# A mixture-of-experts layer on one core: the second product set between the halves of the next expert's first product, and requests held until scatters are issued

## The chip, the cores and the metric

The kernel runs on one core of a Trainium2 chip. The metric is device time in microseconds (us). Times of the kernel before are given as the median of three runs and as one profiled execution.

## The reference

A gated cross-attention block is followed by a gated mixture of experts over 2048 tokens of 256 elements. The change touches the second part alone:

```
logits = xf @ gate_w.T;  probs = sigmoid(logits)
top_vals, sel = top_k(probs, 2)                      # 2 of 16 experts a token
weights = top_vals / (top_vals.sum(-1) + 1e-6)
slot = expert * capacity + rank                      # capacity 320 rows an expert
padded[slot] = x_rep                                 # rows of each expert
h = gelu(einsum('ecd,edf->ecf', padded, w1))         # first product: 256 -> 512
out_padded = einsum('ecf,efd->ecd', h, w2)           # second product: 512 -> 256
out = (out_padded[slot] * weights).sum over the 2 choices
x = x + tanh(g_ffn) * out
```

## The kernel before, in words

Every engine has a program of its own, written out by hand, and semaphores alone tie them together. The first part (attention, router) writes each token's normalised row to the DRAM tensor `padded`, at the place of its expert and rank, with indirect DMAs issued by GpSimd (`dispatch`, L456 to L461). The expert part then loops over e = -4 to 15 on each engine (`expert_steps`, L319), where a step works on several experts at once.

All products take float32 operands in two parts, a high one (rounded to float32r) and a low one (the rest), and sum three of the four partial products (`PARTS`, L1201). So a 128 x 128 block of weights costs three matmuls.

**SyncE** (L371 to L399) asks for the data. `fetch(e)` issues three DMAs for the 320 rows of an expert (into `xg`, which stands in the tile `diag`, 5 buffers). In step e it asks for w2 of expert e + 3 (once the buffer `raw2` is free: w2_low), then w1 of e + 4 (w1_low), then fetches the rows of e + 3. Each waits in order on the one queue. A weight request is 512 KB.

**TensorE** (L1345 to L1419). `first_product` of step e belongs to expert e + 1: four blocks f of the 512 hidden elements, each with 2 x 3 matmuls into its own PSUM bank of `ps_scores`, 24 weight loads (L1370) in all. Ahead of f = 0 and of f = 2 it waits until the results of the expert before have left the first or second two banks (h_low; per expert it counts 2, one a half). `turn` (L1354) transposes the rows of e + 2 in six steps. `second_product` of expert e goes over the rows in three tiles: k = 0 and k = 1 of 128 rows, 12 matmuls each (L1388), and the third of 64 rows (L1398, L1399). It waits for w2_low, for both halves of h (h_low at 2e + 2), and for its output banks (y_last, y_ready). For expert 15 the output goes to banks of `ps_scores` instead.

**ScalarE** (L703 to L750) in step e: gelu of the two halves of e + 1 in place (L713), high part of the rows of e + 2 (L701), high part of w1 of e + 3 (L723), result k = 0 of e scaled by its weight into `y` (the tile `wqT`, L729), high part of w2 of e + 2 (L741), result k = 1 (L729), half of the third (L747). `rows_high`, `result` and `rows_low` are its and VectorE's helpers.

**VectorE** (L1081 to L1121) in step e: for each half of h of e + 1 a high part (L1093) and two low parts (L1095, L1096; the last raises h_low), low part of the rows (L1079), of w1 of e + 3 (L1106; raises w1_low), of w2 of e + 2 (L1110; raises w2_low), and the third result (L1118; raises y_last).

**GpSimd** (L545 to L555) adds the results into the output with indirect DMAs that accumulate, one for each k. Before an expert's first it waits until all three of the expert before have landed (`added`), since two experts may hold the same token; then each waits for its result (y_ready, y_ready, y_last). A memset of one column, `sent`, marks the end of the dispatches (L540).

Of the kernel before, what the change touches and what calls it, by code (L numbers as in the profile page):

```python
# [5 lines left out]
F32 = mybir.dt.float32  # L6
# [58 lines left out]
def exists(t, n=TILES):  # L65

    return 0 <= t < n
# [8 lines left out]
def build(nc, x, ctx_in, mask, g_xattn, g_ffn, ln_gamma, ln_beta, wq, wkv, wo, bo, gate_w, w1, w2, out):  # L76
# [8 lines left out]
    with ExitStack() as held:  # L85
# [36 lines left out]
        sent = sb("sent", [P, 1])  # L122
# [131 lines left out]
        gate_centred, rows_sent = sem("gate_centred"), sem("rows_sent")  # L254
# [61 lines left out]
        def dispatch_done(engine, r):  # L316
            engine.wait_ge(dispatched[r % 2], 64 * (r // 2 + 1))

# [5 lines left out]
        def _(sp):  # L324
# [61 lines left out]
            def expert(e, j, i):  # L386

                n = e + 3
# [3 lines left out]
                n = e + 4  # L392
                if 2 <= n < EXPERTS:
                    sp.wait_ge(w1_low, n - 1)
                    sp.dma_start(raw1[:, n % 2], w1_load[n]).then_inc(w1_loaded[n % 2], 16)
                if e >= -1:
                    fetch(e + 3)
# [4 lines left out]
        def _(pool):  # L402
# [137 lines left out]
            pool.memset(sent[:, :], 0.0).then_inc(rows_sent, 1)  # L540
# [4 lines left out]
            for e in range(EXPERTS):  # L545
# [15 lines left out]
        def _(act):  # L561
# [141 lines left out]
            def expert(e, j, i):  # L703
# [5 lines left out]
                t = e + 1  # L709
                if exists(t, EXPERTS):  # L710
                    for h in range(2):
                        act.wait_ge(h_made, 2 * t + h + 1)
                        act.activation(h_at(t, h), ps_scores[:, 2 * h:2 * h + 2, 0:CAPACITY], ACT.Gelu).then_inc(h_act, 1)  # L713
                if e >= 0:
                    rows_high(e + 2, j)

                t, p = e + 3, (j + 1) % 2
                if exists(t, EXPERTS):
                    act.wait_ge(w1_loaded[p], 16 * (t // 2 + 1))
                    wait(act, h_made, 2 * (t - 1))  # L720
                    if t < 2:
                        act.wait_ge(scored, 2 * TILES)
                    act.activation(w1_hl(p, 0), raw1[:, p], ACT.Copy).then_inc(w1_high, 1)  # L723
# [29 lines left out]
        def _(dve):  # L753
# [327 lines left out]
            def expert(e, j, i):  # L1081
# [5 lines left out]
                t, p = e + 1, (j + 1) % 2  # L1087
                if exists(t, EXPERTS):
                    for h in range(2):
                        fs, n = slice(2 * h, 2 * h + 2), 2 * P  # L1090
                        dve.wait_ge(h_act, 2 * t + h + 1)
                        wait(dve, y_made, SLOT_TILES * (t - 1))
# [9 lines left out]
                if exists(t, EXPERTS):  # L1102
                    if t == 0:
                        dve.wait_ge(rows_sent, 1)
# [338 lines left out]
```

## Time and profile before

| What | us |
| --- | --- |
| Median of 3 runs | 340.29 |
| Range of the runs | 338.02 to 340.69 |
| Profiled execution, device time | 339.9 |
| Its span | 338.2 |
| TensorE busy (matmul) | 308.3 |
| TensorE weight loads busy | 267.3 |
| VectorE busy | 251.2 |
| ScalarE busy | 207.9 |
| GpSimd busy | 191.4 |

The span runs from the first to the last recorded instruction; the device time has 1.7 us more around it. Matmuls (PE) are pipelined and recorded with modelled ends, so the weight loads (PEld), which follow one another, show TensorE's pace better. SPq and POOLq are DMA issues. A timeline row merges like instructions that follow each other (x24). `wqT` is the tile of the results `y`, `diag` that of the gathered rows, `score_t` and `w_third` hold the split weights, `value_t` the split rows and h.

### The profile page before, as it was taken

What the parts mean: (1) busy time and instruction counts of PE and PEld (TensorE: products, weight loads), DVE (VectorE), ACT (ScalarE), POOL (GpSimd) and SP (SyncE); (2) the same over time, 40 slices, a digit from 0 to 9 for tenths busy, and PEclk for the clock granted to TensorE, in tenths of its full rate; (3) what the DMA queues carried; (4) which work ended last, traced back from release to release, by engine and by line L of the source; (5) the groups of instructions that cost most, each with busy time, mean ns of one, the idle gap of its engine ahead of it and who ended that gap; (6) DMA issues with size and microseconds to landing.
All of it is one profiled execution on the core that took longest, in us unless ns stands there. A gap on an engine that the chain in (4) does not pass through costs nothing. (4 is left out here: it accounts for less than half of the span.)

```text
span 338.2 us, 6265 instructions
## 1 busy us (share of the span) xinstructions
PE 308.3 (91%) x2077; PEld 267.3 (79%) x2080; DVE 251.2 (74%) x585; ACT 207.9 (61%) x570; POOL 191.4 (57%) x242
## 2 busy tenths in 40 slices
PE   8989999999999999998849999999999999999800
PEld 3646779988888888887724899999999999999700
DVE  2679887698989898989755398888888888887200
ACT  2646877887888888866461376666666666665300
POOL 8034566585777777788771023555555555566650
PEclk9999999999999999999978999999999999999965
DMA  6989999700111111111224737878787878853440
GB/s 159 274 241 292 182 167 152 195 19 16 49 49 55 57 57 64 56 51 62 78 95 149 249 104 201 204 205 208 204 216 211 224 202 220 211 82 43 48 46 8
DMA packets 40906, 45.68 MB, mean 135 GB/s; under 512 B 5461, under 2 KB 34666, under 8 KB 40874
## 3 DMA queue, kind: packets, MB, share of 16 engines
q1 hardware_dynamic: 33410, 35.78, 39.3%
q0 software_dynamic: 7424, 9.48, 15.6%
q8 instruction: 17, 0.28, 0.4%
q14 instruction: 15, 0.12, 0.2%
q10 hardware_dynamic: 40, 0.02, 0.0%
HBM read 28.02 MB, written 17.24 MB: 134 GB/s over the span
## 5 line engine op out<-in xcount | busy, mean ns | idle before, releaser
L554 POOL DMA_INDIRECT out_dram<-wqT,diag x48 | 73.3, 1528 | 77.4 <-DMA out_dram<-wqT,diag 43.4
L1370 PE MATMUL ps_scores<-value_t,score_t 128*128 128x320 f32 x384 | 59.1, 310 | 0.0
L1370 PEld LDWEIGHTS ps_scores<-value_t,score_t 128*128 128x128 f32 x384 | 56.5, 188 | 0.4 <-DVE value_t L1079 0.3
L1269 PE MATMUL ps_out<-value_t,pT 128*128 128x256 f32 x384 | 53.3, 289 | 0.9 <-DVE pT L968 0.9
L1240 PE MATMUL ps_scores<-score_t,xn 128*128 128x512 f32 x192 | 53.9, 426 | 0.0
L1269 PEld LDWEIGHTS ps_out<-value_t,pT 128*128 128x128 f32 x384 | 47.7, 189 | 1.7 <-issue 1.6
L1240 PEld LDWEIGHTS ps_scores<-score_t,xn 128*128 128x128 f32 x192 | 36.4, 190 | 6.8
L713 ACT ACTIVATE ps_scores<-ps_scores 128x640 f32<-128x640 f32 x30 | 20.6, 688 | 34.2 <-PE ps_scores L1370 34.1
L460 POOL DMA_INDIRECT padded<-z,slot_row x32 | 33.4, 1043 | 10.0 <-issue 7.1
L640 ACT ACTIVATE probs<-ps_scores,row_low 128x64 f32<-128x64 f32 x128 | 38.0, 327 | 0.5 <-DVE row_low L941 0.5
L1093 DVE CAST value_t<-ps_scores 128x640 fp32r<-128x640 f32 x30 | 24.7, 824 | 18.0 <-ACT ps_scores L713 17.8
L492 POOL TENSOR_TENSOR probs<-probs,norm 128x1024 f32<-128x1024 f32 x15 | 28.6, 1906 | 5.5 <-DVE norm L909 5.5
L640 ACT ACTIVATION_READ_ACCUMULATOR probs<-ps_scores,row_low 128x1 f32 x128 | 28.4, 222 | 0.0
L848 DVE TENSOR_TENSOR pT<-ps_pT,pT 128x512 fp32r<-128x512 f32 x28 | 18.5, 660 | 5.2 <-ACT pT L606 4.9
L1095 DVE TENSOR_TENSOR value_t<-ps_scores,value_t 128x512 fp32r<-128x512 f32 x30 | 20.8, 692 | 1.0
L1106 DVE TENSOR_TENSOR score_t<-raw,score_t 128x1024 fp32r<-128x1024 f32 x16 | 19.4, 1216 | 2.6 <-POOL sent L540 2.6
L1193 PE MATMUL ps_misc<-zeros 128*128 128x512 bf16 x62 | 18.8, 461 | 1.5 <-DVE zeros L805 1.2
L1079 DVE TENSOR_TENSOR value_t<-ps_pT,value_t 128x640 fp32r<-128x640 f32 x16 | 13.1, 816 | 8.2 <-ACT value_t L701 8.2
L606 ACT ACTIVATE pT<-ps_pT 128x512 fp32r<-128x512 f32 x32 | 18.0, 644 | 0.9 <-PE ps_pT L1217 0.9
L701 ACT ACTIVATE value_t<-ps_pT 128x640 fp32r<-128x640 f32 x16 | 11.3, 706 | 11.9 <-PE ps_pT L1354 11.7
L630 ACT ACTIVATE gexp<-ps_scores,l 128x16 f32<-128x16 f32 x16 | 4.4, 276 | 22.3 <-PE ps_scores L1256 16.7
L483 POOL CAST xn<-xn_full 128x256 fp32r<-128x256 f32 x16 | 6.4, 399 | 20.6 <-ACT xn_full L654 20.5
(210 smaller groups left out, 690.0 us busy)
## 6 DMA issues: line engine op xcount, KB each, us to landing
raw<-in_L_ffn_w_dram SPq DMA_DIRECT2D x16, 512.0 KB, 4.8
wo_sb<-in_L_ffn_w_dram SPq DMA_DIRECT2D x16, 512.0 KB, 3.5
padded<-empty SPq DMA_DIRECT2D x2, 2064.0 KB, 31.0
diag<-padded SPq DMA_DIRECT2D x16, 258.0 KB, 4.9
out_dram<-x SPq DMA_DIRECT2D x16, 128.0 KB, 1.7
padded<-empty SPq DMA_DIRECT2D x1, 1032.0 KB, 34.1
diag<-padded SPq DMA_DIRECT2D x16, 64.5 KB, 4.7
wq_sb<-in_L_xattn_Wq_dram SPq DMA_DIRECT2D x2, 512.0 KB, 8.0
```

What stands on the lines that cost most here:

```text
L460: pool.indirect_dma_start(padded, bass.IndirectOffsetOnAxis(ap=slot_row[:, r % 2, k, q:q + 1], axis=0), z2[:, (2 * r + k) % RING, q], None ...
L492: pool.tensor_tensor(probs[:, p], probs[:, p], norm[:, p, :, None].to_broadcast([P, HEADS, KEYS]), ALU.mult).then_inc(normed, 1)
L554: pool.indirect_dma_start(out, bass.IndirectOffsetOnAxis(ap=xg[0:SLOTS[k], r, k, TOKEN:TOKEN + 1].bitcast(U32), axis=0), y[0:SLOTS[k], j, ...
L640: op = act.activation(probs[:, j, n], ps_scores[:, 1, at:at + KEYS], ACT.Exp, scale=-1.0, bias=row_low[:, n:n + 1], accum_out=row_sum[:, j ...
L713: act.activation(h_at(t, h), ps_scores[:, 2 * h:2 * h + 2, 0:CAPACITY], ACT.Gelu).then_inc(h_act, 1)
L1093: dve.tensor_copy(h_high_of(p)[:, fs], h_at(t, h)).then_inc(h_high, 1)
L1095: dve.tensor_tensor(h_low_of(p)[:, fs], h_at(t, h)[:, :, 0:n], h_high_of(p)[:, fs, 0:n].bitcast(F32), ALU.subtract)
L1106: dve.tensor_tensor(w1_hl(p, 1), raw1[:, p], w1_hl(p, 0).bitcast(F32), ALU.subtract).then_inc(w1_low, 1)
L1193: pe.matmul(ps_misc[:, :], idle_rows[:, 0:P], idle_rows, start=True, stop=True)
L1240: op = pe.matmul(dst, xn[:, t % 2, a, c], mv, start=False, stop=last)
L1269: op = pe.matmul(ps_attn, pT[:, a, c], mv, start=c == 0 and (a, b) == PARTS[0], stop=c == HC - 1 and (a, b) == PARTS[-1])
L1370: op = pe.matmul(ps_scores[:, f, 0:CAPACITY], w1_hl(p, a)[:, c, f * P:(f + 1) * P], x_hl(p, b)[:, c], start=c == 0 and (a, b) == PARTS[0], ...
```

## The change

- TensorE: for e = 0 to 13 the step is now blocks f = 0, 1 of the first product of e + 1, the turn of e + 2, the second product of e, blocks f = 2, 3 of e + 1. Step 14 does the whole first product of 15 and then the second product of 14; step 15 the second product of 15. The second product starts once the first half of h is split, and asks for the second half ahead of k = 0, f = 2. For expert 15 the waits on y_last and y_ready are gone.
- ScalarE and VectorE: the order of the halves follows (`halves`): half 1 of e, then w1 of e + 2, then half 0 of e + 1, the rows, and so on.
- GpSimd: after an expert's three scatters it writes one column of `sent` and raises a new semaphore, `issued` (experts 0 to 14).
- SyncE: from step 1 on, the rows of e + 3 are fetched first, and only once expert e - 1's scatters are issued; then w1 of e + 4, then w2 of e + 3. In steps before that w1 stands ahead of w2, and the rows last.

```diff
-        sent = sb("sent", [P, 1])
+        sent = sb("sent", [P, EXPERTS])
...
+        def halves(e):
+
+            if e == -1:
+                return ((0, 0), (0, 1))
+            mine = ((e, 1),) if 0 < e < EXPERTS - 1 else ()
+            later = ((e + 1, 0),) if 0 <= e < EXPERTS - 1 else ()
+            return mine + later + (((e + 1, 1),) if e == EXPERTS - 2 else ())
...
             def expert(e, j, i):      # SyncE
 
+                if e >= 1:
+                    sp.wait_ge(issued, e)
+                    fetch(e + 3)
+                n = e + 4
+                if 2 <= n < EXPERTS:
+                    sp.wait_ge(w1_low, n - 1)
+                    sp.dma_start(raw1[:, n % 2], w1_load[n]).then_inc(w1_loaded[n % 2], 16)
                 n = e + 3
                 if 2 <= n < EXPERTS:
                     sp.wait_ge(w2_low, n - 1)
                     sp.dma_start(raw2[:, n % 2], w2_load[n]).then_inc(w2_loaded[n % 2], 16)
-                n = e + 4
-                if 2 <= n < EXPERTS:
-                    sp.wait_ge(w1_low, n - 1)
-                    sp.dma_start(raw1[:, n % 2], w1_load[n]).then_inc(w1_loaded[n % 2], 16)
-                if e >= -1:
+                if -1 <= e < 1:
                     fetch(e + 3)
...
-            pool.memset(sent[:, :], 0.0).then_inc(rows_sent, 1)
+            pool.memset(sent[:, EXPERTS - 1:], 0.0).then_inc(rows_sent, 1)
...
+                if e < EXPERTS - 1:   # GpSimd, behind an expert's three scatters
+                    pool.memset(sent[:, e:e + 1], 0.0).then_inc(issued, 1)
...
+                def first_high(t, p):      # ScalarE
+
+                    if exists(t, EXPERTS):
+                        act.wait_ge(w1_loaded[p], 16 * (t // 2 + 1))
+                        wait(act, h_made, 2 * (t - 1))
+                        if t < 2:
+                            act.wait_ge(scored, 2 * TILES)
+                        act.activation(w1_hl(p, 0), raw1[:, p], ACT.Copy).then_inc(w1_high, 1)
+
+                for t, h in halves(e):
+                    act.wait_ge(h_made, 2 * t + h + 1)
+                    act.activation(h_at(t, h), ps_scores[:, 2 * h:2 * h + 2, 0:CAPACITY], ACT.Gelu).then_inc(h_act, 1)
+                    if e > 0 and t == e:
+                        first_high(e + 2, j)
                 if e >= 0:
                     rows_high(e + 2, j)
+                else:
+                    first_high(e + 3, (j + 1) % 2)
...
-                    pe.wait_ge(h_low, 2 * e + 2)
+                    pe.wait_ge(h_low, 2 * e + 1)
                     for k in range(SLOT_TILES - 1):
-                        if k == 0:
-                            wait(pe, y_last, e)
-                        else:
-                            wait(pe, y_ready, 2 * e)
+                        if e < EXPERTS - 1:
+                            if k == 0:
+                                wait(pe, y_last, e)
+                            else:
+                                wait(pe, y_ready, 2 * e)
                         for f in range(FC):
+                            if k == 0 and f == FC // 2:
+                                pe.wait_ge(h_low, 2 * e + 2)
...
+                elif e < EXPERTS - 2:
+                    first_product(e, j, i, range(FC // 2))
+                    turn(e, j, i)
+                    second_product(e, j, i)
+                    first_product(e, j, i, range(FC // 2, FC))
                 else:
                     first_product(e, j, i)
-                    turn(e, j, i)
                     second_product(e, j, i)
```

VectorE's part changes as ScalarE's does: `first_low` (L1106's split, with the same waits) stands behind half 1 of e, and in steps before 0 at the end of the halves.

## Rows read from the trace of the kernel before

**Rows 1.** The page's slices: busy tenths of TensorE in 40 equal slices.

```profile
PE   8989999999999999998849999999999999999800
```

**Rows 2.** Busy time by stretch: us, each engine (count), PEclk, DMA share, GB/s.

```profile
250.00:260.00 10.00, 10.00 (x78) 9.76 (x77) 8.59 (x13) 6.26 (x11) 4.55 (x3) 1.00 0.75 184
...
330.00:338.00 8.00, 0.00 (x0) 0.00 (x0) 0.00 (x0) 0.00 (x0) 0.00 (x0) 0.50 0.05 6
```

**Rows 3.** Who waited for whom, 195 to 325 us: total us, times, longest.

```profile
POOL out_dram L554 <- DMA out_dram<-wqT,diag: 43.4, 15, 5.5
...
PE ps_scores L1388 <- DVE wqT L1118: 1.3, 1, 1.3
```

**Rows 4.** Timeline, one period of the weight loads: start us, us, engine, line, operation.

```profile
250.56 3.53 PEld L1370 LDWEIGHTS ps_scores<-value_t,score_t 128*128 128x128 f32 x24
...
254.99 1.49 PEld L1388 LDWEIGHTS ps_out<-score_t,value_t 128*128 128x128 f32 x12
...
258.79 3.53 PEld L1370 LDWEIGHTS ps_scores<-value_t,score_t 128*128 128x128 f32 x24
```

**Rows 5.** Timeline: the last split of the results of that first product.

```profile
256.59 0.28 DVE L1096 TENSOR_TENSOR value_t<-ps_scores,value_t 128x128 fp32r<-128x128 f32 x1
```

**Rows 6.** Timeline of GpSimd, first to last scatter: [idle before, releaser].

```profile
178.37 0.12 POOL L540 MEMSET sent<- 128x1 f32 x1
...
200.63 1.62 POOL L554 DMA_INDIRECT out_dram<-wqT,diag  x1 [22.14 <-ACT wqT L729]
...
202.55 2.03 POOL L554 DMA_INDIRECT out_dram<-wqT,diag  x1 [0.31 <-issue]
...
260.78 1.56 POOL L554 DMA_INDIRECT out_dram<-wqT,diag  x1 [3.18 <-DMA out_dram<-wqT,diag]
...
286.00 1.56 POOL L554 DMA_INDIRECT out_dram<-wqT,diag  x1 [3.92 <-DMA out_dram<-wqT,diag]
...
304.97 1.42 POOL L554 DMA_INDIRECT out_dram<-wqT,diag  x1 [0.31 <-issue]
...
308.79 1.56 POOL L554 DMA_INDIRECT out_dram<-wqT,diag  x1 [2.40 <-DMA out_dram<-wqT,diag]
...
316.51 1.56 POOL L554 DMA_INDIRECT out_dram<-wqT,diag  x1 [2.55 <-DMA out_dram<-wqT,diag]
...
324.07 1.56 POOL L554 DMA_INDIRECT out_dram<-wqT,diag  x1 [2.40 <-issue]
```

**Rows 7.** Timeline of the last two experts.

```profile
308.04 3.53 PEld L1370 LDWEIGHTS ps_scores<-value_t,score_t 128*128 128x128 f32 x24
...
311.53 1.51 PEld L1388 LDWEIGHTS ps_out<-w_third,value_t 128*128 128x128 f32 x12
...
313.37 0.47 ACT L729 ACTIVATE wqT<-ps_out,diag 128x256 f32<-128x256 f32 x1 [0.81 <-PE ps_out L1388]
...
316.83 2.93 PEld L1388 LDWEIGHTS ps_scores<-score_t,value_t 128*128 128x128 f32 x24 [1.44 <-issue]
```

**Rows 8.** Timeline of the first expert.

```profile
196.59 0.50 PEld L1354 LDWEIGHTS ps_pT<-ident,diag 128*128 128x128 f32 x4
...
198.29 1.38 SPq L381 DMA_DIRECT2D diag<-padded  x1
...
199.31 0.48 ACT L729 ACTIVATE wqT<-ps_out,diag 128x256 f32<-128x256 f32 x1
...
201.90 1.22 DVE L1110 TENSOR_TENSOR w_third<-wo_sb,w_third 128x1024 fp32r<-128x1024 f32 x1
```

**Rows 9.** Stretches of 0.6 us around the first requests, then one request's issue.

```profile
199.60:200.20 0.60, 0.60 (x7) 0.60 (x6) 0.60 (x3) 0.60 (x2) 0.00 (x0) 1.00 1.03 352
...
200.80:201.40 0.60, 0.60 (x7) 0.60 (x6) 0.60 (x2) 0.36 (x1) 0.60 (x1) 1.00 0.07 22
...
259.89 0.37 SPq L391 DMA_DIRECT2D wo_sb<-in_L_ffn_w_dram  x1
```

**Rows 10.** DMA issues of the page: median us from issue to landing.

```profile
diag<-padded SPq DMA_DIRECT2D x16, 258.0 KB, 4.9
```

More of the change, by code:

```diff
@@ L253, in build @@
         consts, diag0, idle_ready = sem("consts"), sem("diag0"), sem("idle_ready")
-        gate_centred, rows_sent = sem("gate_centred"), sem("rows_sent")
+        gate_centred, rows_sent, issued = sem("gate_centred"), sem("rows_sent"), sem("issued")
         filled, out_act, out_dve = sem("filled"), sem("out_act"), sem("out_dve")
@@ L1085, in expert, with first_low @@
                         rows_low(n, n)
[L1087 to L1092, printed above, removed]
-                        dve.tensor_copy(h_high_of(p)[:, fs], h_at(t, h)).then_inc(h_high, 1)
-                        dve.wait_ge(h_high, 2 * t + h + 1)
-                        dve.tensor_tensor(h_low_of(p)[:, fs], h_at(t, h)[:, :, 0:n], h_high_of(p)[:, fs, 0:n].bitcast(F32), ALU.subtract)
-                        dve.tensor_tensor(h_third(p)[:, fs, SLOTS[2]:], h_at(t, h)[:, :, n:], h_high_of(p)[:, fs, n:].bitcast(F32),
-                                          ALU.subtract).then_inc(h_low, 1)
+                def first_low(t, p):
+                    if exists(t, EXPERTS):
+                        if t == 0:
+                            dve.wait_ge(rows_sent, 1)
+                        dve.wait_ge(w1_high, t + 1)
+                        dve.tensor_tensor(w1_hl(p, 1), raw1[:, p], w1_hl(p, 0).bitcast(F32), ALU.subtract).then_inc(w1_low, 1)
@@ new lines, in expert @@
+                for t, h in halves(e):
+                    fs, n, p = slice(2 * h, 2 * h + 2), 2 * P, t % 2
+                    dve.wait_ge(h_act, 2 * t + h + 1)
+                    wait(dve, y_made, SLOT_TILES * (t - 1))
+                    dve.tensor_copy(h_high_of(p)[:, fs], h_at(t, h)).then_inc(h_high, 1)
+                    dve.wait_ge(h_high, 2 * t + h + 1)
+                    dve.tensor_tensor(h_low_of(p)[:, fs], h_at(t, h)[:, :, 0:n], h_high_of(p)[:, fs, 0:n].bitcast(F32), ALU.subtract)
+                    dve.tensor_tensor(h_third(p)[:, fs, SLOTS[2]:], h_at(t, h)[:, :, n:], h_high_of(p)[:, fs, n:].bitcast(F32),
+                                      ALU.subtract).then_inc(h_low, 1)
+                    if e > 0 and t == e:
+                        first_low(e + 2, j)
@@ L1098, in expert @@
                 if e >= 0:
                     rows_low(e + 2, j)
-                t, p = e + 3, (j + 1) % 2
-                if exists(t, EXPERTS):
-                    if t == 0:
-                        dve.wait_ge(rows_sent, 1)
-                    dve.wait_ge(w1_high, t + 1)
-                    dve.tensor_tensor(w1_hl(p, 1), raw1[:, p], w1_hl(p, 0).bitcast(F32), ALU.subtract).then_inc(w1_low, 1)
+                else:
+                    first_low(e + 3, (j + 1) % 2)
                 for t in SPLIT_W2.get(e, (e + 2,)):
@@ L1355, in turn, with first_product @@
                     op.then_inc(xg_turned, 1)
-            def first_product(e, j, i):
+            def first_product(e, j, i, fs=range(FC)):
                 t, p = e + 1, (j + 1) % 2
@@ L1362, in first_product @@
                     pe.wait_ge(w1_low, t + 1)
-                    for f in range(FC):
+                    for f in fs:
                         if e == -1 and f == FC // 2:
```

13 lines of the change are left out of this document (1 added, 12 removed).

## The prediction

> **What bounds the kernel now.** Three views, in this order: the slices of the page, the chain of work that ended last, the timeline of the expert stage. In the slices TensorE is full in all but a few slices from the 23rd to the 37th [rows 1], and a stretch of 10 us in mid-stage shows it busy all the time at a granted clock of 1.00, which is 2.4 GHz [rows 2]. The timeline gives its period: the first product's 24 weight loads of one expert begin at 250.56, the next one's at 258.79, 8.2 us apart, with 3.53 us for the first product and the rest turning rows and second product [rows 4]. Nothing between has a stall.
>
> That alone does not set the end. The chain of waits ends on GpSimd's scatters. Each expert has three; the first waits until all three of the expert before have landed, 43.4 us over 15 waits [rows 3]. A round is 5.15 us from the first issue to the end of the third, then the landing: 3.18 us beside loads (260.78), 3.92 at worst (286.00), 2.40 once no load is left (304.97 + 1.42 = 306.39 to 308.79) [rows 6]. So a free round takes 7.56 us (316.51 to 324.07) and a loaded one about what TensorE takes. GpSimd starts expert 0 at 200.63, 0.84 us after that expert's first result is copied (199.31 + 0.48 = 199.79) [rows 6, 8]. At expert 14 it is late: the result is there at 313.37 + 0.47 = 313.84, so the scatter could go at 314.7, and it goes at 316.51 [rows 6, 7]. Expert 15's scatter (324.07) waits for that round and not for TensorE. From 324.07 to the end, 338.2, is 14.1 us that the change does not touch: one round, its landing, and an empty stretch [rows 2, 6].
>
> So what counts is one instant, the start of expert 14's scatters: the later of (a) GpSimd's own row of rounds and (b) the first result of expert 14.
>
> **The change, part by part.** Half a first product is 12 of its 24 loads, 3.53 / 2 = 1.77 us [rows 4]; call the halves A and B.
>
> 1) *Order on TensorE, experts 0 to 13.* Before: A, B of e+1, turn, second product of e. After: A of e+1, turn, second product of e, B of e+1. The instructions are the same ones, so the period stays 8.2; each second product comes 1.77 us earlier. Expert 0's goes from 197.52 (end of the turn that begins at 196.59) to 195.8, its first scatter from 200.63 to 198.9 [rows 6, 8].
>
> 2) *New waits in the period.* B of e now ends just before A of e+1, and its results must be through ScalarE and VectorE when the second product reaches its third quarter. Rows: the loads of a first product end at 250.56 + 3.53 = 254.09, its last split on VectorE at 256.59 + 0.28 = 256.87, so 2.78 us [rows 4, 5]. TensorE gets there after A (1.77), the turn (0.9, 254.09 to 254.99) and six loads of the second product (0.7): 3.4 us. Margin 0.6, so I cost it at nothing; if VectorE were 1 us late it would cost 0.4 a period. VectorE has the same work in a period as before (8.59 us busy in 10 us [rows 2]), and the diff puts the split that is needed ahead of w1's, so I take it as free when B ends.
>
> 3) *The hand-over to the last two experts.* Here the reordering stops: expert 14's step does A and B of 15 together, then the second product of 14. TensorE comes to A of 15 at the old time, 308.04, since it has done the same work by then [rows 7]. But B of 14 has only just ended, and B of 15 writes the banks that it filled: it must wait for h_low = 30, which comes 2.78 after 308.04, at 310.8. A of 15 ends at 309.8. **A new stall of about 1.0 to 1.1 us.** Below it is bounded by 0 (if results drained in A's time), above by the whole 2.78. I take 1.05, as the drain is a row. So B of 15 ends at 308.04 + 2.78 + 0.1 + 1.77 = 312.7, where the second product of 14 used to start at 311.53.
>
> 4) *The removed waits of expert 15* (y_last, y_ready): before, TensorE stood still from 315.4 to 316.83 (the trace counts 1.3 of it) [rows 3, 7]. A second product is 3.8 (254.99 to 258.79 [rows 4]), so after the change 15's follows at 312.7 + 3.8 = 316.5, 0.3 earlier than before. Worth nothing: expert 15's scatter waits for a landing.
>
> 5) *Requests behind the scatters.* Before, the two weight loads and the rows left just ahead of a round (259.89 for the round of 260.78) and ran beside its third scatter's packets [rows 6, 9]. After, the rows leave when the third scatter is issued and the weights behind them, w1 only once its buffer is split (about 2 us later). The third scatter has its landing nearly to itself. I take 2.4 to 3.2 for the landing, so a round of 7.6 to 8.35 with TensorE's 8.2 as the floor: GpSimd keeps up or falls back by 0.1 a round. The added memset costs 0.12 [rows 6] and lies in the landing. SP waits in order, so w1, w2 and rows are all held by one wait; the rows are needed 8 us later and land in about 4.9 [rows 10], the weights later still.
>
> 6) *Order of requests at the start.* The w2 of expert 3 (512 KB), which before went out in step 0 as soon as its buffer was free, now stands between w1 of 4 and the rows of 3, which wait for VectorE. In the old trace those rows were requested up to 198.29 and the queues were empty by 200.8 [rows 8, 9]. Add 0.5 to issue and 512 KB at 352 GB/s, 1.5 us: 202.8; scatters run beside them. The turn of expert 3 wants them at 203.1. Bounds 0 to 1 us of stall, I take 0.
>
> **What speaks against it.** The one loaded round whose scatter stood beside VectorE's two-input subtract shows 2.03 us for it (202.55, beside the split at 201.90 to 203.12) where the others take 1.56 [rows 6, 8]. After the change the w2 split falls on every round's second scatter, by my order of VectorE's work (split about 6.8 to 8.0 us behind the end of B, second scatter 7.5 behind it), so 0.47 a round is possible: 5.6 + 2.4 = 8.0, still under 8.2, but with a 3.18 landing it is 8.8. The Trainium skill (SBUF — State Buffer, "SBUF: two separate sides") says that VectorE with two SBUF inputs and GpSimd take one port pair as a lock, in which the loser waits for the whole instruction. By that rule each such scatter is held; the trace agrees in one case of one.
>
> **The sum.** First result of 14 copied: 312.7 + (313.84 - 311.53 = 2.31) = 315.0. Plus 0.84: scatter at 315.85, where it was 316.51: -0.7 us. GpSimd's own row gets there only if its lag behind TensorE at expert 13 exceeds 2.6 us (now: second product at 308.04 - 3.8 = 304.2, plus 2.3 and 0.84 gives 307.4, and the scatter goes at 308.79, 1.4 late). Then 7.56 and 14.1 unchanged: span 337.5. The profiled execution took 339.9 with a span of 338.2, so **339.2 us**. The runs shown have a median of 340.29, range 338.02 to 340.69. With (b) in charge at 314.7 the old kernel would give 338.1, near its best run, so I read its spread as GpSimd's lag, which the changed kernel no longer passes on; therefore I keep 339.2 and do not add the 0.4 between its profile and median.
>
> **The rivals.**
> R1, *the new stall does not appear or is hidden* (drain in A's time). For: nothing but that VectorE has less to do at the end. Against: rows 5. Then the result of 14 comes 1.05 earlier, the scatter at 314.8: 338.2 us.
> R2, *GpSimd's rounds become the bound* (slower side). Place: the rounds of experts 0 to 11, beside the loads that now start while scatters are in flight. 198.9 + 12c + 2 x 7.56 must exceed 315.85, so it decides from c = 8.5 us a round. With 5.15 + 0.47 + 3.18 = 8.8: 319.6 against 316.51, +3.1, 343.0 us. With the worst landing, 3.92, and no lock, c = 9.1: 346.6. For: the 2.03 row, the 3.92 row. Against: the loads avoid the landing now.
> R3, *TensorE waits for rows or for a drain*: one stall of 1 at expert 3, or 0.1 to 0.2 in each of 13 periods. +1 to +2.5 on the forecast: 340.2 to 341.7. Against: the margins above.
> R4, *no effect*: if the stall is 1.7 instead of 1.05, 339.9.
>
> **How the numbers follow.** Forecast with R4 0.53 (338.7 to 339.9), R1 0.12, R3 0.14, R2 0.16, something that I don't see 0.05. A measurement of this kernel tells about 1% (3.4 us) from no change. Faster by over 1% needs 336.9: no case gives it; it gets the unseen 0.05. Slower by over 1% (343.7) is the upper part of R2, two thirds of its 0.16: 0.11. Within 1%: the rest, 0.84. The range takes in R1 and R3 and leaves most of R2 out: 337.6 to 341.9.
>
> **What would show it.** Right: second product of 0 near 195.8; TensorE's period 8.2; a gap of 1 us in the first product of 15; no gap ahead of 15's second product; scatters of 14 about 0.9 behind the copy; landings of 2.4 to 3. Wrong: a round over 8.5, scatters over 1.6 us in every round, TensorE idle at turns, or no gap at 15.

## The result: slower by 0.6%, where 0.2% faster was forecast

| | before | changed |
|---|---|---|
| median of 20 runs (range), us | 339.3 (338.02 to 340.69) | 341.33 (339.90 to 342.89) |
| ratio, 95% interval | 1 | 1.0057 (1.0041 to 1.0072) |
| profiled execution / its span, us | 339.9 / 338.2 | 342.02 / 340.2 |

Forecast was 339.2 us, 0.7 less than the profiled execution of before (0.1 less than the median of its 20 runs); the measured median is 2.1 above the forecast. It lies in the range (337.6 to 341.9) and under the 1% that the chances were about, but it moved the other way. Here and below medians and ranges take in all executions, while the ratios leave out those over 1.5% above the fastest of the same kernel.

The page's row of TensorE, 8.5 us a slice, over the changed kernel's span:

```profile
PE   8989999999999999999859998999999999999900
```

One slice in the expert stage that was full before is no longer: the 25th (204.1 to 212.6 us) shows 8, and the forecast had no stall there. In the middle of the stage TensorE and its clock are as they were [rows 2]:

```profile
core 0: us, PE busy (x) PEld busy (x) DVE busy (x) ACT busy (x) POOL busy (x), PEclk, DMA share, GB/s
...
250.00:260.00 10.00, 10.00 (x79) 9.76 (x79) 8.53 (x14) 6.75 (x11) 5.81 (x5) 1.00 0.79 196
```

The list of waits (engine, tile and line that waited, what for, us in total, times, longest) shows GpSimd as forecast and TensorE not:

```profile
POOL out_dram L565 <- ACT wqT L745: 62.3, 14, 20.2
...
POOL out_dram L565 <- DMA out_dram<-wqT,diag: 3.4, 2, 3.1
...
PE ps_pT L1373 <- DMA diag<-padded: 2.0, 1, 2.0
```

Before, the scatters of all experts but the first waited for a landing (15 waits in the list [rows 3]). Now 14 of the 16 rounds wait for a result (before: one), which is what "GpSimd keeps up" means. The two that still wait for a landing are expert 9's, 3.1 us, and expert 15's at 326.00 below, 2.31 us. In both kernels the list has the one of expert 15 under "issue", and counts as a landing one gap of 0.3 us (320.24 before, 322.15 now) such as stands ahead of the second and third scatter of every round. The last line is new: once, TensorE's turn of rows waits 2.0 us for rows to land. The timeline has the place, expert 3's rows (SPq is SyncE's DMA queue, L402 requests w1, L406 w2, L386 to L389 the rows):

```profile
197.09 0.37 SPq L402 DMA_DIRECT2D raw<-in_L_ffn_w_dram  x1
...
197.50 1.55 SPq L406 DMA_DIRECT2D wo_sb<-in_L_ffn_w_dram  x1
...
199.10 0.51 SPq L386 DMA_DIRECT2D diag<-padded  x1
...
199.13 1.62 POOL L565 DMA_INDIRECT out_dram<-wqT,diag  x1 [20.21 <-ACT wqT L745]
...
200.17 0.60 SPq L389 DMA_DIRECT2D diag<-padded  x1
...
205.54 0.42 PEld L1373 LDWEIGHTS ps_pT<-ident,diag 128*128 128x128 f32 x4 [2.21 <-issue]
```

The rows of expert 3 were requested from 197.25 before; now w1 of 4 and w2 of 3 stand ahead, the issue of w2 alone holds SyncE for 1.55 us, and the first of them leaves at 199.10. By the landing events of the two traces they land at 205.44 (before: 202.66). TensorE is ready to turn them at 203.33 (205.54 less the gap of 2.21), 1.5 us earlier than before (204.79), since the second product is moved ahead. A spare 2.1 us has become a stall of 2.2.

The other new gap is where it was forecast, in the first product of expert 15. The timeline of the last two experts, to be held against [rows 7] (each row's stretch merges what has no gap in it; the x24 at 308.95 is the second half of 14 and the first half of 15):

```profile
308.95 3.53 PEld L1389 LDWEIGHTS ps_scores<-value_t,score_t 128*128 128x128 f32 x24
...
313.55 1.78 PEld L1389 LDWEIGHTS ps_scores<-value_t,score_t 128*128 128x128 f32 x12 [1.06 <-DVE value_t L1118]
315.28 1.53 PEld L1410 LDWEIGHTS ps_out<-w_third,value_t 128*128 128x128 f32 x12
...
318.41 1.57 POOL L565 DMA_INDIRECT out_dram<-wqT,diag  x1 [4.88 <-ACT wqT L745]
...
326.00 1.57 POOL L565 DMA_INDIRECT out_dram<-wqT,diag  x1 [2.31 <-issue]
```

The scatters of 14 start at 318.41 where 315.85 was forecast. The 2.56 between them: first product of expert 0 begins 0.25 later in this execution (second product of 0 at 196.00 for 195.75), the stall at expert 3 gives 2.2, twelve periods of 8.23 for 8.21 give 0.24, and the hand-over comes out 0.1 better. From 318.41 on it is 7.59 to expert 15 and 14.2 to the end, as before.

### The profile page after: what moved, and what is told of

Same layout as the page of the kernel before. It is cut to its first block and busy times, and to the rows that moved or that the text cites. A ratio compares the mean times of both kernels' runs of the same rounds, so it can differ in the third digit from the quotient of the medians.

```text
span 340.2 us, 6310 instructions
## 1 busy us (share of the span) xinstructions
PE 309.8 (91%) x2080; PEld 267.7 (79%) x2080; DVE 250.9 (74%) x585; ACT 209.3 (62%) x570; POOL 193.1 (57%) x257
## 5 line engine op out<-in xcount | busy, mean ns | idle before, releaser
L1115 DVE CAST value_t<-ps_scores 128x640 fp32r<-128x640 f32 x30 | 24.6, 822 | 20.7 <-ACT ps_scores L733 20.7
```

Source lines behind the costliest of these rows:

```text
L1115: dve.tensor_copy(h_high_of(p)[:, fs], h_at(t, h)).then_inc(h_high, 1)
```

## The experiments

Fourteen runs, in four groups: twelve new kernels, the changed kernel again and one of the twelve again. Each ratio is against the kernel of before, run in the same group on the same chip (23 to 35 runs, medians 339.1 to 339.8). The profiled executions vary: the first product of expert 0 begins anywhere from 187.5 to 190.2, so places in the expert stage are compared within a profile.

**The old order of requests in the first steps** (`first_order_old`): w2 of 3 ahead of w1 of 4 again; from step 1 on as changed.

```diff
+                if e < 1:
+                    n = e + 3
+                    if 2 <= n < EXPERTS:
+                        sp.wait_ge(w2_low, n - 1)
+                        sp.dma_start(raw2[:, n % 2], w2_load[n]).then_inc(w2_loaded[n % 2], 16)
                 n = e + 4
...
                 n = e + 3
-                if 2 <= n < EXPERTS:
+                if e >= 1 and n < EXPERTS:
```

> Edit: in steps before 1 SyncE asks in the old order (w2 of e + 3, w1 of e + 4, rows), so the w2 of expert 3 no longer stands between w1 of 4 and the rows of 3; all else as in the changed kernel. Theory T1 (the 2.2 us that TensorE waits for the rows of expert 3, requested at 199.1 where they were at 197.25, move everything behind them): the rows are asked for near 197.4, the turn of expert 3 starts without a wait, the scatters of 14 start 2.2 earlier: about 339.1 us, ratio to before 0.997 to 1.002. Rival R2 (GpSimd's rounds or the traffic beside them set the end): the wait goes and the time stays above 340.5. Rival R5 (the rows are late because expert 0's scatters, now earlier, take the DMA engines, and the order of requests is only in part the cause): a wait of 0.5 us or more remains, 339.7 to 340.8.

Measured: 340.7 us (12 runs, 339.17 to 344.2), ratio 1.0039 (1.0011 to 1.0067). Its profiled execution, 339.17 us, has no wait for rows: they are requested from 196.82 and TensorE turns them without a gap. The scatters of 14 go at 315.51. The trace agrees with T1. The median does not: the ratio is above T1's 0.997 to 1.002, on the side of R2 (above 340.5), and its interval overlaps that of the changed kernel. One profile, of the fastest execution, does not say what the slower ones wait for. So the rows of 3 were taken up once more, below.

**The requests undone** (`requests_undone`): SyncE's part and the memset as before, TensorE's, ScalarE's and VectorE's new order kept.

```diff
-                if e >= 1:
-                    sp.wait_ge(issued, e)
-                    fetch(e + 3)
+                n = e + 3
+                if 2 <= n < EXPERTS:
+                    sp.wait_ge(w2_low, n - 1)
+                    sp.dma_start(raw2[:, n % 2], w2_load[n]).then_inc(w2_loaded[n % 2], 16)
                 n = e + 4
...
-                if -1 <= e < 1:
+                if e >= -1:
                     fetch(e + 3)
```

> Edit: SyncE's part and the memset that raises issued go back to the kernel before; TensorE, ScalarE and VectorE keep the new order. T1 with my accounting (the end is the first result of expert 14 plus 0.84, whatever GpSimd's lag up to 2.6 us): no wait for the rows of 3, scatters of 14 about 0.9 behind the copy, 339.1 us, the same as first_order_old; requests behind scatters are worth nothing here. If GpSimd's landings beside loads matter after all, its lag at expert 13 exceeds 2.6 us and the time is 340 or more.

Measured: 341.48 us (12 runs), ratio 1.0060 (1.0033 to 1.0086). This was not expected. Its timeline shows rows of a later expert that are late now:

```profile
262.61 1.74 SPq L386 DMA_DIRECT2D diag<-padded  x1
...
269.75 0.42 PEld L1368 LDWEIGHTS ps_pT<-ident,diag 128*128 128x128 f32 x4 [1.47 <-issue]
```

The new order on TensorE asks for rows 1.77 us earlier in every period. From the landing events to the turns, before had 1.8 to 4.2 us to spare for the rows of experts 4 to 14, this kernel 0.1 to 1.7 in ten of the eleven and three at 0.1, of which one waited 1.5, the changed one 2.1 to 5.8. The two parts of the change belong together: the rows ahead of the weights, behind the scatters, give the margin back that the new order takes. With this part undone, the stall moves to another expert. The profiled execution took 340.1, 1.4 less than the median; that the slower ones have more such stalls is likely and not shown.

**The requests alone** (`requests_alone`): the kernel of before with SyncE's part and the memset of the changed one; the engines' order is the old one.

```diff
+                if e >= 1:
+                    sp.wait_ge(issued, e)
+                    fetch(e + 3)
...
-                if e >= -1:
+                if -1 <= e < 1:
                     fetch(e + 3)
...
+                if e < EXPERTS - 1:
+                    pool.memset(sent[:, e:e + 1], 0.0).then_inc(issued, 1)
```

> Edit: the kernel before with the change's requests and memset only (order on TensorE, ScalarE, VectorE as before). Theory: rows of 3 asked for at about 199, landing near 205.5, where TensorE wants them at 204.8: a wait of 0.6 to 0.8. GpSimd's rounds then follow the results with landings of 2.4 to 2.9, so its 1.8 us of lag at expert 14 is gone: scatters of 14 at 314.7 + 0.7 = 315.4 against 316.5, so 338.2 us, ratio 0.995 to 0.999. Rival (requests behind scatters do not free the landing): lag of 1.5 or more at 14 and a wait at 3 on top, 340 us.

Measured: 340.57 us (12 runs), ratio 1.0031 (1.0010 to 1.0053). No gain, where 338.2 was expected; GpSimd still trails TensorE by 1.8 us at expert 14. The wait for the rows of 3 that was expected is not in its profile: they land at 205.05 and are turned at 206.36. The timeline shows one thing that holds GpSimd (L557 is the scatter, L1115 VectorE's subtract of w2, 1024 columns, both inputs in SBUF):

```profile
243.87 1.22 DVE L1115 TENSOR_TENSOR score_t<-wo_sb,score_t 128x1024 fp32r<-128x1024 f32 x1
...
244.48 2.05 POOL L557 DMA_INDIRECT out_dram<-wqT,diag  x1 [2.46 <-ACT wqT L734]
246.83 1.57 POOL L557 DMA_INDIRECT out_dram<-wqT,diag  x1 [0.30 <-issue]
...
260.33 1.22 DVE L1115 TENSOR_TENSOR score_t<-wo_sb,score_t 128x1024 fp32r<-128x1024 f32 x1
...
261.24 1.74 POOL L557 DMA_INDIRECT out_dram<-wqT,diag  x1 [2.37 <-DMA out_dram<-wqT,diag]
```

A scatter that starts while the subtract runs takes longer, the longer the earlier in it it started, and ends 1.44 us behind the subtract's end (245.09 to 246.53; 261.55 to 262.98). Eight scatters of this profile start inside such a subtract, and seven of them are longer (the eighth starts 0.03 us before its end). This is the one case of [rows 6, 8], 2.03 us, met in numbers. It is not all of the lag: from expert 8 on no scatter is held, and GpSimd trails by 1.4 to 2.5 and waits up to 3.8 us for a landing.

**The split kept at step 14** (`half_kept_at_14`): the changed kernel, but the last two experts are interleaved like the others, which trades the 1.05 stall ahead of the second product of 14 for one behind it.

```diff
-            mine = ((e, 1),) if 0 < e < EXPERTS - 1 else ()
+            mine = ((e, 1),) if 0 < e < EXPERTS else ()
...
-            return mine + later + (((e + 1, 1),) if e == EXPERTS - 2 else ())
+            return mine + later
...
-                elif e < EXPERTS - 2:
+                elif e < EXPERTS - 1:
```

> Edit: in the changed kernel step 14 keeps the new order too (A of 15, second product of 14, B of 15, then the second product of 15; half 1 of 15 is drained in step 15). Theory T2 (the wait of 1.06 and B of 15, 1.77, stand ahead of the second product of 14 and so ahead of the end): the scatters of 14 start 2.5 earlier (0.3 of a wait for the half of 14 remains inside its second product), a wait of about 2 us appears inside the second product of 15 but its result still comes at about the landing of 14's scatters: 341.3 - 2.5 = 338.8 us, ratio to before 0.996 to 1.001. Rival: TensorE's new wait sets the end instead, the scatters of 15 wait for its result, 339.5 or more; or the wait for rows at expert 3 grows.

Measured: 339.98 us (12 runs, 337.5 to 345.5), ratio 1.0001 (0.9976 to 1.0025). Its profiled execution was one of the long ones (343.74). The new gap is 2.05 us in the second product of 15, and the scatters of 15 wait for the round of 14 anyway. The ratio, in which three of the twelve (343.74 to 345.5) don't count, is clear of the changed kernel's 1.0057 (1.0041 to 1.0072), although the wait at the turn of 3 is still there (1.74 us): the order of the last two experts is worth about as much as that wait. What it gives when GpSimd is late is less, as the next kernels show.

**The changed kernel again** (`changed_again`), in one group with the next three.

> The changed kernel itself, beside the next three on one chip, for their base and for a second profile. Every theory: ratio to before 1.004 to 1.007. T1 (rows of expert 3): the wait at the turn of 3 is there again, 1.5 to 2.5 us.

Measured: 342.6 us (6 runs), ratio 1.0084 (1.0057 to 1.0112), with the same wait: `PE ps_pT L1373 <- DMA diag<-padded: 1.6, 1, 1.6`.

**The rows of 3 first** (`rows3_first`, and in another group `rows3_first_again`): in step 0 alone, the fetch stands ahead of the two weight requests.

```diff
+                if e == 0:
+                    fetch(e + 3)
                 if e >= 1:
                     sp.wait_ge(issued, e)
                     fetch(e + 3)
...
-                if -1 <= e < 1:
+                if e == -1:
                     fetch(e + 3)
```

> Edit: in step 0 SyncE asks for the rows of expert 3 ahead of the two weight requests. T1: no wait at the turn of 3, its rows there 5 us or more before it; the time falls by 1.5 to 2.3 against changed_again. T3 (beside that wait, the new order has left each turn less time for its rows, 2.1 to 3 us where it was 3.1 to 4.2, and in runs with a late DMA TensorE waits again): the fall is smaller, about 1, and the ratio to before stays at 1.002 to 1.005.

> rows3_first once more, as the base of the run before it and for a second profile. T1: no wait at the turn of 3, ratio to before 0.999 to 1.002. Whether TensorE waits at later turns, as it did four times in the first profile, is open: T3 expects at least one such wait or a late landing.

Measured: 339.56 us (12 runs), ratio 1.0005 (0.9985 to 1.0024), beside 1.0084 of the changed kernel in the same group; the intervals are far apart. The 3.0 us between the medians are more than the stall of 2 and than the 1.5 to 2.3 of T1; `changed_again` has six runs only. Again: 339.7 us (12 runs), 1.0019 (0.9997 to 1.0041). The timeline of the second:

```profile
186.93 0.59 SPq L386 DMA_DIRECT2D diag<-padded  x1
...
202.14 0.51 PEld L1375 LDWEIGHTS ps_pT<-ident,diag 128*128 128x128 f32 x4
```

Measured from the first product of expert 0 the rows leave 11 us earlier than they did, and the turn of expert 3 has no gap. The wait at this turn is in all three profiles that have the new order on TensorE and the w2 of 3 between the w1 of 4 and these rows (2.21, 1.87 and 1.74 us) and in no other, and one fetch moved takes the loss away in two groups: **the cause of the loss is shown.** Later in the same profile one landing is late, and GpSimd is held after it (L1131 is the subtract of w2, L1111 that of w1):

```profile
288.90 1.22 DVE L1131 TENSOR_TENSOR score_t<-wo_sb,score_t 128x1024 fp32r<-128x1024 f32 x1
...
289.24 2.32 POOL L567 DMA_INDIRECT out_dram<-wqT,diag  x1 [3.75 <-ACT wqT L747]
...
293.63 1.22 DVE L1111 TENSOR_TENSOR score_t<-raw,score_t 128x1024 fp32r<-128x1024 f32 x1
...
293.74 2.41 POOL L567 DMA_INDIRECT out_dram<-wqT,diag  x1 [0.30 <-issue]
```

Two of the round's three scatters are held, by 0.75 and 0.99 us (the third takes 1.42 when free), and the next round starts 9.4 later instead of 8.2. At expert 13 GpSimd is 1.8 behind its place. From the second product of 13 to that of 14 it is 10.1 us instead of 8.2, since all of 15's first product and its stall stand between; that takes the lag up, and the scatters of 14 go at 315.06, 3.13 behind the start of their second product, as in the changed kernel.

A lag of 1.8 costs nothing here. A longer one does, by another way: the rows are asked for only when the scatters of an expert are issued. In the first profile of `rows3_first`, an execution of 341.86, a landing takes 4.23 us at expert 10, GpSimd trails by 3.8, and the rows of expert 14 leave late:

```profile
284.59 1.57 POOL L567 DMA_INDIRECT out_dram<-wqT,diag  x1 [4.23 <-DMA out_dram<-wqT,diag]
...
290.48 0.37 SPq L386 DMA_DIRECT2D diag<-padded  x1
...
294.94 0.42 PEld L1375 LDWEIGHTS ps_pT<-ident,diag 128*128 128x128 f32 x4 [1.67 <-issue]
```

They land at 294.83. With 0.87 us more at the turn of 15, TensorE stands 2.5 us, which is what this execution has over the median of its group (2.3). So T3 holds for a part of the executions.

**All rows ahead of the scatters** (`rows_before_scatters`): `fetch(e + 3)` in every step first, ahead of the wait for the scatters' issue; and the same with the split kept at step 14 (`rows_before_scatters_half_kept`).

```diff
-                if e >= 1:
-                    sp.wait_ge(issued, e)
-                    fetch(e + 3)
+                if e >= 0:
+                    fetch(e + 3)
+                if e >= 1:
+                    sp.wait_ge(issued, e)
```

> Edit: rows3_first, and from step 1 on the rows of e + 3 are asked for before the wait on issued, the weights still behind it. The rows then land 5 us or more before their turn. T3: about 1 us faster than rows3_first, ratio to before 0.997 to 1.001, and a narrower spread. Rival (what is left over is not the rows but the scatters, which are late in some runs, or the order on TensorE itself): the same as rows3_first within 0.3 us, or slower if rows beside the third scatter delay its landing.

> Edit: rows_before_scatters, and step 14 keeps the new order (A of 15, second product of 14, B of 15). T2: the scatters of 14 start about 2.5 earlier; then the result of 15, behind B of 15 and a wait of about 2.2 for its drain, comes at about the same time as the landing of 14's scatters: 2 to 2.5 us below rows_before_scatters, ratio to before 0.990 to 0.994. Rival (the last results set the end and take back most of it): 1 us or less.

Measured: 339.91 us (11 runs, 338.98 to 340.49), ratio 1.0006 (0.9991 to 1.0022); and 339.3 us (11 runs), 0.9992 (0.9976 to 1.0008). T3 expected a narrower spread, which came (1.5 us where `rows3_first` has 3.7), and about 1 us less, which did not (0.35 more). The second kernel misses the 0.990 to 0.994 of T2 and is 0.6 below the first, as its rival has it. Rows have 5 to 8 us to spare and TensorE never waits for them in the two profiles, but they run beside the scatters again, GpSimd trails by 1.8 to 2.0 from expert 6 on, and 9 and 11 scatters are held by a subtract. In the second, expert 14's scatter goes at 314.79, 5.35 behind the start of its second product (309.44), where the two level kernels with this split (below) need 3.74: without the stall at 14 the lag of 1.6 is what is paid instead.

**The rows of 3 first and the split kept** (`rows3_first_half_kept`).

> Edit: rows3_first (rows of expert 3 ahead of the weights in step 0, later rows still behind the scatters) and step 14 keeps the new order. Theory T4 (with the rows before the scatters GpSimd ran 1.9 us behind its results from expert 6 on and so took back most of the 3.1 that half_kept frees; with the rows behind them it ran level in the changed kernel's profile): scatters of 14 follow the result by 0.9, 2.0 to 2.5 below rows3_first_again: ratio to before 0.992 to 0.996. Rival (in most executions a late landing makes GpSimd trail here too, as in the profile of rows3_first): 0.3 to 1.0 us below, ratio 0.997 to 1.000.

Measured: 339.47 us (12 runs, 337.12 to 341.75), ratio 1.0000 (0.9972 to 1.0029). That is T4's rival (0.997 to 1.000), and 0.2 below `rows3_first_again`. But five of the twelve are between 337.1 and 338.1, the others near 340. The profiled execution is one of the five, 337.12: GpSimd level throughout, no scatter held, expert 14's at 313.54, with the gap of 2 us where it does no harm (weight loads of 15's second product):

```profile
313.54 1.57 POOL L567 DMA_INDIRECT out_dram<-wqT,diag  x1 [2.67 <-ACT wqT L747]
...
318.58 3.20 PEld L1412 LDWEIGHTS ps_scores<-score_t,value_t 128*128 128x128 f32 x18 [2.05 <-DVE value_t L1120]
...
321.13 1.57 POOL L567 DMA_INDIRECT out_dram<-wqT,diag  x1 [2.30 <-DMA out_dram<-wqT,diag]
```

Two groups of times from one kernel would follow from a small margin: while GpSimd is level, its first scatter starts 0.46 us ahead of the w2 subtract (in the changed kernel 300.02 and 300.48) and is not held; once a landing is half a us late, it starts inside it, is held, and stays late. Only an execution of the faster group has a profile, so that the others run in this way is a guess. The last four kernels test the hold.

**The subtracts cut** (`splits_cut`): `rows_before_scatters_half_kept` with VectorE's low parts of w1 (from expert 2) and w2 (from expert 3) made for 64 of 1024 columns. It leaves out most of the low parts of those weights; nothing else changes in number or order. And the same cut in `requests_alone` (`requests_alone_splits_cut`).

```diff
-                        dve.tensor_tensor(w2_hl(t % 3, 1), raw2[:, t % 2], w2_hl(t % 3, 0).bitcast(F32), ALU.subtract
+                        n = (1, 64) if t >= 3 else (FC, DIM)
+                        dve.tensor_tensor(w2_hl(t % 3, 1)[:, 0:n[0], 0:n[1]], raw2[:, t % 2, 0:n[0], 0:n[1]], w2_hl(t % 3, 0)[:, 0:n[0], 0:n[1]].bitcast(F32), ALU.subtract
```

> Edit: rows_before_scatters_half_kept, and VectorE's low parts of w1 (from expert 2) and of w2 (from expert 3) are computed for 64 of their 1024 columns alone, so most low parts of the weights are left out. T5 (a scatter that GpSimd starts while VectorE runs one of these subtracts of two SBUF inputs is held until the subtract ends, 0.3 to 1.0 us longer, and that keeps GpSimd 1.8 us behind): no scatter over 1.65 us, GpSimd level with its results from expert to expert, scatters of 14 near 3.15 behind the start of the second product of 14, 1.5 to 2 us below rows_before_scatters_half_kept: ratio to before 0.992 to 0.996. Rival T6 (GpSimd trails because its landings are slow beside the loads, 3 us or more): scatters are 1.57 but the lag stays above 1.2 and the ratio is 0.997 to 1.000.

> Edit: requests_alone (old order on all engines, requests behind the scatters) with the low parts of the weights cut in the same way. T5 (7 of its first scatters in a round started inside a subtract and took about 2.05, so the requests freed nothing there): no scatter over 1.65, 1 to 2 us below requests_alone: ratio to before 0.995 to 0.999. T6: 1.001 to 1.004, as with the splits whole.

Measured: 337.67 us (6 runs, 337.12 to 338.08), ratio 0.9930 (0.9907 to 0.9953), where the uncut kernel had 0.9992 (0.9976 to 1.0008) in its group: clearly faster, and the spread is down to 1 us. All 48 scatters are short, 73.0 us together. In `requests_alone` the cut brings 339.73 us (12 runs), 1.0000 (0.9981 to 1.0019) from 1.0031 (1.0010 to 1.0053): the same direction, with intervals that overlap and a value between those of T5 and T6, so unclear. No scatter is held there either, but GpSimd still waits for late landings (15.1 us in 6 waits, up to 4.1) and trails by 1.2 at expert 14 where it was 1.8. What the cut changes is seen from round to round: after a late landing GpSimd now gains 0.7 us in the next round, where in `requests_alone`, with the first scatters of experts 2 to 5 held, it stayed 1.1 to 1.2 behind. Shorter subtracts also leave VectorE less to do, which this pair does not take apart from the hold; the next kernel keeps all the work.

**The w2 subtract moved** (`w2_split_moved`): `rows3_first_half_kept`, complete in its work, with VectorE's subtract of w2 of e+1 right behind that of w1 of e+2, ahead of the second half's results, in place of w2 of e+2 at the end of the step. And the same with all rows ahead of the scatters (`w2_split_moved_rows_early`).

```diff
                     if e > 0 and t == e:
                         first_low(e + 2, j)
+                        second_low(e + 1)
...
-                for t in SPLIT_W2.get(e, (e + 2,)):
...
+                if e == -2:
+                    for t in range(2):
+                        second_low(t)
```

> Edit: rows3_first_half_kept, and VectorE splits w2 of e + 1 right behind w1 of e + 2 (it split w2 of e + 2 behind the rows): both subtracts then stand where a level GpSimd waits for a landing. T5: a scatter can be late by 1.5 us, not 0.5, before it is held, so late executions recover: median 337.3 to 338.3 (ratio 0.993 to 0.997) where rows3_first_half_kept had 1.000. T6: the same 1.000 as before the edit. Rival: TensorE waits for the rows' low part, which now ends 1.2 later in the period: a wait at each first product and 340 or more.

> Edit: rows_before_scatters_half_kept with the same move of w2's split. T5: fewer scatters held than the 11 in the profile of rows_before_scatters_half_kept; if the traffic of the early rows still makes GpSimd trail by more than 1.5, the third scatter meets w1's split and the gain stays small: ratio 0.993 to 0.999. T6: 0.999, as without the move.

Measured: 337.88 us (8 runs, 336.78 to 344.48), ratio **0.9951 (0.9914 to 0.9988)**: faster than before, by 0.5%, and than the changed kernel. Against `rows3_first_half_kept` (1.0000, 0.9972 to 1.0029, in another group) the intervals overlap a little, so what the move alone gives is likely, not shown, and two of the eight executions (341.05 and 344.48) still stand apart. Its timeline shows the subtracts between two rounds:

```profile
243.79 1.42 POOL L567 DMA_INDIRECT out_dram<-wqT,diag  x1 [0.30 <-issue]
...
245.24 1.22 DVE L1111 TENSOR_TENSOR score_t<-raw,score_t 128x1024 fp32r<-128x1024 f32 x1
246.37 1.22 DVE L1117 TENSOR_TENSOR score_t<-wo_sb,score_t 128x1024 fp32r<-128x1024 f32 x1
...
248.28 1.57 POOL L567 DMA_INDIRECT out_dram<-wqT,diag  x1 [2.95 <-ACT wqT L747]
```

The last scatter of a round is issued by 245.21, both subtracts run to 247.59, the next round starts at 248.28. None of its 48 scatters is held, and expert 14's goes at 313.83. No landing is late in this profile, so it does not show a late one being made good. TensorE has no wait for the rows' low part, which the rival had named. With rows early it is 339.62 us (12 runs), 0.9990 (0.9963 to 1.0016), which T5 and T6 both allow: landings beside the rows (waits of 3.8 and 4.3 us ahead of experts 5 and 6) make GpSimd late by more than the new margin, and eight third scatters are held (1.71 to 2.10 us), seven by w1's subtract, which now has w2's right behind it, and one by w2's. By the medians, where the subtracts stand and what the landing runs beside are worth something only together.

## Why the prediction was wrong

Point by point, by its own steps:

- *Step 1, order on TensorE.* Right: second product of 0 at 196.00 (195.8), period 8.23 (8.2).
- *Step 2, new waits in the period.* Right: no gap in any of the middle periods.
- *Step 3, the hand-over.* Right: 1.06 us of stall by the timeline, 1.05 forecast. R1, that it doesn't appear, is out.
- *Step 4, removed waits.* Right: 15's second product follows at 319.13 with no gap, and its scatter waits for a landing.
- *Step 5, requests behind the scatters.* Right for the changed kernel: GpSimd is level from expert 1 to 14, but for one landing of 3.1 from which it recovers in the next round, so R2 did not happen there. The memset shows 0.62, not 0.12, inside the landing, at no cost.
- *Step 6, requests at the start.* **This is the step that failed.** It gave bounds of 0 to 1 us, took 0, and the stall is 2.2 by the timeline, 1.9 in `changed_again` (2.0 and 1.6 in the lists of waits). The mechanism was named, and R3 priced it at "one stall of 1 at expert 3" with a chance of 0.14 and a time of 340.2 to 341.7; 341.33 lies in it. The term that was mis-sized most is the old landing. It was read off a window with a DMA share near 0 at 200.8 [rows 9]; by the landing events those rows landed at 202.66, 1.9 later. With the other two terms as they stand (0.5 for the issue, 1.5 for 512 KB) that gives 204.7 against a turn ready at 203.3, a stall of 1.3. The rest is in the two terms: 205.44 was measured. The request was put at 0.5 us later and was 1.85, as the issue of w2 took 1.55; but in `changed_again` no issue is long, the request is 0.5 later when measured from the first product of expert 0 (1.6 in the first profile), and the rows land 7.1 us behind it. So the stall does not need the long issue; it comes with the weights ahead. The recorded rows had a warning: the last rows are issued from 198.29 [rows 8], and 4.9 us from issue to landing [rows 10] gives 203.2 even with nothing moved, against a turn that wants them at 203.1.

*What spoke against it.* The hold of a scatter by the subtract is real, and what the Trainium skill (SBUF — State Buffer, "SBUF: two separate sides") says of a lock, in which the second to start waits for the whole instruction of the first, fits the scatters: those that start first are not held, those that start second end 1.44 to 1.46 us (the third of a round 1.30) behind the subtract's end. It does not fit the subtract: started 0.46 us into a scatter of 1.57, it takes its usual 1.22 (300.48), so the scatter does not keep it out. The place in the forecast was wrong too: the hold was put on every round's second scatter, and in the changed kernel it is on none. It matters once GpSimd is late. With the rows ahead of the scatters it keeps GpSimd 1.8 to 2.0 us behind, and with the subtracts cut GpSimd is level; in `requests_alone` it is 0.5 of the 1.8, by one profile each.

*The readings of before.* Its spread was taken as GpSimd's lag, to be gone after the change. The changed kernel, with GpSimd level in its profiles, spreads by 3.0 us as before did by 2.7. Part of it lies ahead of the experts (187.5 to 190.2 for the first product). This reading was wrong, though it moved the forecast by no more than 0.4. Two small ones: the slices from the 23rd to the 37th all show 9, with no exception, and one of the 15 waits of [rows 3] is no landing but a gap of 0.3.

With step 6 mended the kernel comes near the forecast, 339.56 and 339.7 us for the rows of 3 first against 339.2, but not by the whole sum: the gain of 0.7 on before is in neither of the two ratios (1.0005 and 1.0019). Part of it was the starting point, a profiled execution 0.6 above the median of 20. The profile of `rows3_first_again` has some of the gain: with its first product of expert 0 at 187.78, 0.91 ahead of before's, its scatter of 14 stands at 315.06 + 0.91 = 315.97 by before's clock (forecast 315.85, before 316.51), but the last round takes 7.68 for 7.56 and the end 14.4 for 14.1.

What stays open: what makes a single landing late in some executions and not in others; and whether moving the subtract takes away what such a landing costs afterwards, which the ratios suggest and no profile shows.

## What to carry to other kernels

Before a product is moved ahead, list every transfer that its step needs with the landing time from the trace and the new time it is wanted; a fall in DMA share is no landing, and a request moved behind another one waits for that one's issue and comes in behind its bytes. Look most closely at the first and last turns of a loop, where requests and order follow rules of their own: the period was right to 0.1 us and one fetch in step 0 cost all of the loss. A request that waits for a slower engine makes that engine's delays its own, as the rows behind late scatters did. And a queue that is level by half a us only does not stay so in every execution; here the version with the long two-input VectorE instructions between the bursts of scatters was the fastest complete one.

## What the runs showed of the hardware

- A GpSimd scatter that starts inside VectorE's 128x1024 subtract from two SBUF tiles takes up to 2.61 us (240.73 in `rows_before_scatters`) for 1.42 to 1.57, and ends 1.44 to 1.46 us (the third of a round 1.30) behind the subtract. The sixteen profiles have 54 such scatters; no other takes over 1.62. Two at the edges took the usual time: one that started 0.02 us after the subtract (290.60 in `requests_undone`) and one 0.03 us before its end (294.48 in `requests_alone`). A subtract that starts 0.46 behind the scatter is not lengthened (300.02 and 300.48).
- Issuing one DMA on SyncE takes 0.36 to 0.7 us in 1157 of 1216 cases (all sixteen profiles, from 178 us on) and over 1 us in 48, up to 2.0; all that stands behind it is late by that. What makes it long wasn't found: it was 1.38 us in [rows 8], 1.55 at 197.50 in the changed kernel, with a DMA share of 0.00 in the 1.5 us before, and 1.74 at 262.61 in `requests_undone`.
- From their first request to their last landing event, the rows of experts 4 to 15 take 3.4 to 5.0 us in the changed kernel, where they leave ahead of the weights. Before, behind the weights, those of experts 3 to 14 took 5.4 to 7.1, and the rows of expert 3 behind 1 MB of weights took 6.3 in the changed kernel and 7.1 in `changed_again`.
